# A graph-network kernel on one core: edge counts built in groups of 18 targets instead of 25, one PSUM bank each, five steps' low one-hots in one instruction

## What is computed

```python
h = relu(layernorm(x)); x = x + relu(segment_sum((h @ W0)[src] * edge_weight, dst))        # layer 0
h = relu(layernorm(x)); x = x + relu(segment_sum(norm * (h @ W1.T + b1)[src], dst))        # layer 1, norm from degrees
h = relu(layernorm(x)); x = x + relu((h + segment_sum(h[src], dst)) @ G1 + g1) @ G2 + g2   # layer 2
h = relu(layernorm(x)); x = x + attention over each node's edges, 8 heads of 64            # layer 3
```

## Time and profile before

| | us |
|---|---|
| runs shown | 3061.95, 3048.1, 3062.45 (median 3061.95) |
| the profiled execution's own time | 3038.2 |
| its span, first to last instruction | 3036.9 |
| PE matmuls busy in the span | 2486.5 (82%) |
| VectorE busy | 1823.3 (60%) |
| ScalarE busy | 568.3 (19%) |
| GpSimd busy | 966.9 (32%) |
| granted TensorE clock, mean | 0.914 of full speed |

### The profile page before, as it was taken

How to read it: one execution, slowest core, us unless ns; L and a number is a source line. 1 busy time by engine, 2 the same in 40 slices (tenths; PEclk the granted TensorE clock), 3 DMA queues, 4 the chain that set the end, 5 groups by cost and what they waited for, 6 DMA issues and landing times.

```text
span 3036.9 us, 38594 instructions
## 1 busy us (share of the span) xinstructions
PE 2486.5 (82%) x10085; PEld 1423.8 (47%) x10085; DVE 1823.3 (60%) x4888; ACT 568.3 (19%) x946; POOL 966.9 (32%) x1004
## 2 busy tenths in 40 slices
PE   7888888788777779999899999981288598888777
PEld 5544444434444445666555655640277443333332
DVE  7756577685788884665343334440266377777666
ACT  4533310000255440000000000010266100000000
POOL 0466666666100000000000000017400466666665
PEclk9899998899888889999999999985599689999999
DMA  6686656656231113446211121111134467776665
GB/s 160 185 239 178 176 164 173 171 168 185 76 104 53 62 54 86 113 110 178 76 55 52 52 62 56 34 52 29 43 116 125 125 176 206 207 236 193 190 195 171
DMA packets 154302, 386.19 MB, mean 127 GB/s; under 512 B 43712, under 2 KB 45113, under 8 KB 154115
## 3 DMA queue, kind: packets, MB, share of 16 engines
q0 software_dynamic: 74368, 232.68, 27.0%
q1 hardware_dynamic: 79064, 149.75, 17.1%
q10 hardware_dynamic: 683, 1.28, 0.2%
HBM read 330.88 MB, written 52.72 MB: 126 GB/s over the span
## 4 chain that ended last, share of the span: by engine, by line
PE 52%; DVE 21%; issue 10%; another core or an unknown queue 7%; DMA 6%; POOL 2%; ACT 1%; SPq 0%; ACTq 0%; DVEq 0%
PE banks L1845 18%; PE banks L1983 15%; PE banks L1811 7%; DVE spare L1035 4%; PE banks L2160 3%; DVE spare L1034 3%; PE banks L1975 3%; DMA ring<-edge_counts 3%; POOL ring L2331 2%; DMA ring<-table,src_t 2%; DVE sel L1108 2%; PE banks L1800 1%; DVE rstd L888 1%; PE banks L2063 1%
## 5 line engine op out<-in xcount | busy, mean ns | idle before, releaser
L1845 PE MATMUL banks<-ring,sel 128*125 128x512 f32 x1682 | 877.2, 649 | 156.6 <-issue 112.4
L2264 POOL DMA_INDIRECT ring<-table,src_t x440 | 435.2, 989 | 243.6 <-issue 104.4
L2298 POOL DMA_INDIRECT big<-score_table,src_t x104 | 98.4, 946 | 1291.2 <-DMA score_table<-node_scores 1256.0
L1845 PEld LDWEIGHTS banks<-ring,sel 128*125 128x125 f32 x1682 | 283.0, 196 | 466.6 <-issue 463.6
L2331 POOL DMA_INDIRECT ring<-table,src_t x401 | 384.8, 960 | 226.2 <-issue 98.6
L1983 PE MATMUL banks<-acc,ring 125*125 125x512 f16 x1900 | 438.2, 381 | 7.0 <-issue 7.0
L1975 PE MATMUL banks<-spare 128*125 128x325 f16 x1080 | 276.0, 370 | 73.4 <-DVE spare L1035 20.7
L1983 PEld LDWEIGHTS banks<-acc,ring 125*125 125x125 f16 x1900 | 257.1, 137 | 160.5 <-issue 27.4
L1587 DVE TENSOR_TENSOR ring<-ring,banks 128x512 f32<-128x512 f32 x388 | 255.4, 682 | 119.3 <-DMA ring<-table,src_t 91.9
L1975 PEld LDWEIGHTS banks<-spare 128*125 128x125 f16 x1080 | 152.0, 147 | 197.5 <-issue 194.9
L1436 DVE TENSOR_REDUCE big<-banks 128x16 f32<-128x448 f32 x168 | 101.6, 619 | 198.3 <-remote 139.9
(11 more groups left out here) (409 smaller groups left out, 2936.9 us busy)
## 6 DMA issues: line engine op xcount, KB each, us to landing
ring<-edge_counts SPq DMA_DIRECT2D x38, 683.6 KB
edge_counts<-big SPq DMA_DIRECT2D x25, 683.6 KB
ring<-table,src_t POOLq DMA_INDIRECT x841
sel<-edge_counts SPq DMA_DIRECT2D x12, 683.6 KB
acc<-dst_places SPq DMA_DIRECT2D x28, 256.0 KB
x<-dst_places SPq DMA_DIRECT2D x27, 256.0 KB
table<-stage SPq DMA_DIRECT2D x25, 224.0 KB
x<-in_x SPq DMA_DIRECT2D x25, 224.0 KB
```

The source lines that it names most:

```text
L1845: last = P.matmul(to, sel[:, n % SELS, :], rows, start=False, stop=True, skip_group_check=True)
L2264: G.indirect_dma_start(out=ring[:, i % RING, :], out_offset=None, in_=table[0][:, :], in_offset=bass.IndirectOffsetOnAxis(ap=src_t[:, i:i ...
```

## The change

- GT = 7 groups for each tile, of 18 targets and a last one of 17: 175 groups, 590 steps (BRS, the steps of one of five rows of step tables, 118 instead of 108).
- The key one-hot is 25 x 18 = 450 wide and fits one bank: one matmul a step. Four single banks in turn (MADE = 4) instead of two pairs.
- HOTS = 10. The low one-hots lie side by side; VectorE makes five steps' of them in one TENSOR_TENSOR of 5 x 125 against `low_t` of five steps, with a semaphore of its own, `low_ok`, for which PE waits at every fifth step.
- PE loads its registers GROUP_STEPS = 10 steps at a time, since 590 is no multiple of 20.
- ScalarE counts 174 boundaries (34 first, 14 after each tile), loads 7 registers for each tile, and copies and zeroes 450 columns (18 or 17 of every 18 copied).
- The boundaries' biases (two instructions instead of one) and the rooms of the group tables move.

```diff
-    GT = 5
-    GW_N = TN // GT
+    GT = 7
+    GW_N = -(-TN // GT)
+    GW_LAST = TN - (GT - 1) * GW_N
...
-    HALF_W = HALF_S * GW_N
-    KEY_W = 2 * HALF_W
-    HOTS = 7
+    KEY_W = TILES * GW_N
+    HOTS = 10
+    GROUP_STEPS = 10
+    MADE = 4
...
-    COUNTS_FIRST, COUNTS_EACH = 24, 10
+    COUNTS_FIRST, COUNTS_EACH = 34, 14
...
-        key_hot = [flat_spare[:, n * HOT_W:n * HOT_W + KEY_W // 2].bitcast(F16) for n in range(HOTS)]
-        low_hot = [flat_spare[:, n * HOT_W + KEY_W // 2:(n + 1) * HOT_W].bitcast(F16)[:, 0:TN] for n in range(HOTS)]
+        key_hot = [flat_spare[:, n * KEY_W // 2:(n + 1) * KEY_W // 2].bitcast(F16) for n in range(HOTS)]
+        low_room = flat_spare[:, HOTS * KEY_W // 2:HOTS * KEY_W // 2 + HOTS * TN // 2].bitcast(F16).rearrange("p (n i) -> p n i", i=TN)
+        low_hot = [low_room[:, n, :] for n in range(HOTS)]
...
-            return banks[:, 2 * n:2 * n + 2, 0:HALF_W]
+            return banks[:, n % MADE, 0:KEY_W]
...
-                V.tensor_scalar(out=low_hot[j % HOTS], in0=low_names, scalar1=low_t[:, j:j + 1], scalar2=None, op0=ALU.is_equal).then_inc(hot_ok, 1)
+                if j % LB == 0:
+                    if j >= HOTS:
+                        V.wait_ge(built, j - HOTS + LB)
+                    V.tensor_tensor(low_room[:, j % HOTS:j % HOTS + LB, :], low_names[:, None, :].to_broadcast([128, LB, TN]),
+                                    low_t[:, j:j + LB, None].to_broadcast([128, LB, TN]), ALU.is_equal).then_inc(low_ok, 1)
...
-                    pair = made_bank((n + 1) % 2)[0:TN]
-                    A.copy(made16[t % MAKES][0:TN, :, :, q * GW_N:(q + 1) * GW_N], pair.rearrange("p h (s r) -> p h s r", r=GW_N)).then_inc(taken, 1)
-                    if n + 2 >= GROUPS:
+                    made = made_bank(n + 1)[0:TN]
+                    width = GW_N if q < GT - 1 else GW_LAST
+                    A.copy(made16[t % MAKES][0:TN, :, q * GW_N:q * GW_N + width], made.rearrange("p (s r) -> p s r", r=GW_N)[:, :, 0:width]).then_inc(taken, 1)
+                    if n + MADE >= GROUPS:
...
-                if j % LOADED_TILES == 0:
-                    P.reg_load(tile_regs, group_row[0:1, j:j + LOADED_TILES])
+                if j % GROUP_STEPS == 0:
+                    P.reg_load(tile_regs[0:GROUP_STEPS], group_row[0:1, j:j + GROUP_STEPS])
...
-                P.wait_ge(hot_ok, 2 * (j + 1))
+                P.wait_ge(hot_ok, j + 1)
+                if j % LB == 0:
+                    P.wait_ge(low_ok, j // LB + 1)
                 P.wait_ge(room, v)
-                for h in range(2):
-                    to = banks[0:TN, bass.ds((v & 1) * 2 + h, 1), 0:HALF_W].rearrange("p a d -> p (a d)")
-                    last = P.matmul(to, low_hot[j % HOTS], key_hot[j % HOTS][:, h * HALF_W:(h + 1) * HALF_W],
-                                    start=False, stop=True, skip_group_check=True)
-                last.then_inc(built, 1)
+                to = banks[0:TN, bass.ds(v & (MADE - 1), 1), 0:KEY_W].rearrange("p a d -> p (a d)")
+                P.matmul(to, low_hot[j % HOTS], key_hot[j % HOTS], start=False, stop=True, skip_group_check=True).then_inc(built, 1)
```

More of the change, by code:

```diff
@@ L99, in build @@
     LOADED_TILES = 20
[L100 removed]
+    assert BRS * BRB == BSTEPS and 0 < GW_LAST <= GW_N and KEY_W <= 512 and BSTEPS % GROUP_STEPS == 0 and E // CE == CHUNKS - 1 and TILES == 5 * HQ
     Z_NORM = (D + 1.3) ** 0.5
@@ L254, in build @@
         acc16 = flat_acc.bitcast(F16).rearrange("p (t c) -> p t c", c=2 * D)
-        made16 = [big[:, n * MAKE_W:(n + 1) * MAKE_W].bitcast(F16).rearrange("p (h s r) -> p h s r", h=2, r=TN) for n in range(MAKES)]
+        made16 = [big[:, n * MAKE_W:(n + 1) * MAKE_W].bitcast(F16)[:, 0:TILES * TN].rearrange("p (s r) -> p s r", r=TN) for n in range(MAKES)]
         slot16 = [flat_ring[:, n * SLOT_W:(n + 1) * SLOT_W].bitcast(F16)[:, 0:TILES * TN] for n in range(SLOTS - 1)]
@@ L285, in build @@
         place_of_tile, tile_product = (flat_spare[:, n * gsq:(n + 1) * gsq].rearrange("p (a b) -> p a b", b=TILES) for n in range(2))
-        gap = 2 * gsq
+        gap, each = 2 * gsq, GROUPS + 1
         first_n = flat_spare[:, gap:gap + GROUPS + 1]
-        steps_n, chunk_p, steps_p, end_p, first_p, shift_p, base_p = (
-            flat_spare[:, gap + (n + 1) * 128:gap + (n + 1) * 128 + GROUPS] for n in range(7))
-        first_i = flat_spare[:, gap + 8 * 128:gap + 8 * 128 + GROUPS + 1].bitcast(I32)
-        prior = flat_spare[:, gap + 9 * 128:gap + 9 * 128 + GROUPS]
+        first_i = flat_spare[:, gap + each:gap + 2 * each].bitcast(I32)
+        steps_n, chunk_p, steps_p, end_p, first_p, shift_p, base_p, prior = (
+            flat_spare[:, gap + (n + 2) * each:gap + (n + 2) * each + GROUPS] for n in range(8))
         begun_g, weighed_g = (flat_spare[0:BRS, n * BRB * GROUPS:(n + 1) * BRB * GROUPS].rearrange("p (b g) -> p b g", g=GROUPS) for n in range(2))
-        assert BRB * GROUPS == gsq and gap + 10 * 128 <= 6 * D - EROW
+        assert 2 * BRB * GROUPS <= gap + 3 * each and gap + 10 * each <= 6 * D
         sums = [spare[0:TN, n, :] for n in range(2)]
@@ L652, in vector_program @@
             own.mark(V.tensor_copy(gstep_f[:, :], gstep_i[:, :]))
-            V.tensor_scalar(out=group_bias, in0=node_iota[:, 0:GROUPS - 1], scalar1=-float(GW_N), scalar2=0.5 - GW_N, op0=ALU.mult,
-                            op1=ALU.add).then_inc(consts, 1)
+            starts = group_start.rearrange("p (t q) -> p t q", q=GT)
+            own.mark(V.tensor_scalar(out=starts, in0=node_iota[:, 0:TILES, None].to_broadcast([128, TILES, GT]), scalar1=-float(TN), scalar2=0.5,
+                                     op0=ALU.mult, op1=ALU.add))
+            V.wait_ge(v_own, own.n)
+            V.scalar_tensor_tensor(out=starts, in0=node_iota[:, None, 0:GT].to_broadcast([128, TILES, GT]), scalar=-float(GW_N), in1=starts,
+                                   op0=ALU.mult, op1=ALU.add).then_inc(consts, 1)
             def step_tables():
@@ L1955, in tensor_program @@
             P.wait_ge(keys_ok, BRB + 1)
-            for pair in (1, 0):
-                P.matmul(bank[2 * pair][0:TN, 0:HALF_W], zeros, wide[:, 0:HALF_W], start=True, stop=True)
-                P.matmul(bank[2 * pair + 1][0:TN, 0:HALF_W], zeros, wide[:, 0:HALF_W], start=True, stop=True).then_inc(room, 1)
+            for v in range(1, MADE + 1):
+                P.matmul(bank[v % MADE][0:TN, 0:KEY_W], zeros, wide[:, 0:KEY_W], start=True, stop=True).then_inc(room, 1)
             for j in range(BSTEPS):
-                if j % LOADED_TILES == 0:
-                    P.reg_load(tile_regs, group_row[0:1, j:j + LOADED_TILES])
+                if j % GROUP_STEPS == 0:
+                    P.reg_load(tile_regs[0:GROUP_STEPS], group_row[0:1, j:j + GROUP_STEPS])
                 if j == 16:
```

21 lines of the change are left out of this document (11 added, 10 removed).

## The result

| | before | changed |
|---|---|---|
| median of the runs taken side by side, us | 3058.38 (4 runs, 3048.1 to 3062.45) | 3105.4 (4 runs, 3094.92 to 3106.03) |
| the profiled execution's own time | 3038.2 | 3094.92 |
| count stage, first to last step | 791.1 to 1144.6: 353.5 | 811.5 to 1198.5: 387.0 |
| TensorE's register loads in it | 27, 42.6 us | 59, 122.5 us |

The ratio is 1.0151 [1.0116, 1.0186]: 47 us slower, where +82 was predicted. Of the 57 us between the two profiled executions the count stage holds 33.5, its later start 20, and the rest of the program 3.

A forecast was written before the change was run, and what follows sets the result against it. TensorE's instruction queue was taken to bound the count stage: 236 + 12 + 26 + 141 + 15 = 430 us against 354, +76, and +6 before it, +82 on a median of 3,061.95 made 3,144 us; range 3,060 to 3,170.

The forecast's parts named there:

- rival B: Count stage: long loads cost a fixed surcharge, 2.66 us each; stage 368, in all +20 us, 3,082; chance 0.11.
- The bound: Count stage: TensorE's instruction queue is the bound, at about 0.54 us a step in the kernel before.
- Steps at 0.40, 0.14 for the second matmul: Count stage: one matmul fewer saves 0.14 us a step; 590 steps at 0.40 make 236 us, 56 less.
- The new wait, +12: TensorE's queue: every fifth step also waits on low_ok, 118 instructions of about 0.10 us, +12 us.
- Register loads, 26 + 141 = 167: TensorE's 59 loads of ten: 30 short at 0.88 us, 29 long at 4.86; from 38 to 167 us.
- What lengthens them: TensorE loads of 2.5 to 2.97 us occur where they meet ScalarE's loads; +3 us.
- Left over, 15: Count stage: four banks remove 11.6 us of zeroing waits, the other 12 stay, meeting loads add 3; together 15.
- VectorE hidden: Count stage: VectorE needs 0.39 us a step, 233 plus 11 us, below the stage's 430; costs nothing.
- ScalarE hidden: Count stage: ScalarE's copies and loads take 267 us, below the stage's 430; hidden.
- Before the stage, +6 within 0 to 12: Stage before the count: VectorE's longer permutations add 8.4 us, partly absorbed; +6 us, bounds 0 and 12.
- A: Count stage: loads of ten are cheap on TensorE, 26 us in place of 141; stage 315, run 3,029; chance 0.20.
- C: Count stage: wide one-hots lose their quick form and VectorE becomes the bound; stage 440, run 3,155; chance 0.05.

The follow-up runs named there:

- e2: Kernel before, with TensorE's register loads cut from 20 to 10 steps and nothing else; 3128.36 us, ratio 1.0217 to the kernel before.
- e1: Changed kernel, with TensorE loading 20 steps' registers at a time instead of 10; 3032.67 us, ratio 0.9923 to the kernel before.
- e7: e1, with each matmul of 450 columns cut into two of 225; 2777.2 us, ratio 1.0217 to the kernel before.
- e5: Changed kernel, with TensorE's registers loaded in 88 loads of 1 to 20 and ScalarE's loads as in e3; 2780.82 us in one run.
- e3: e1, with ScalarE's group ends 8 apart, so each load begins on a multiple of 32 bytes; 3031.76 us, ratio 0.9918 to the kernel before.
- e6: e1, with narrow one-hots made step by step again and no wait for low_ok; 2686.47 us, ratio 0.9885 to the kernel before.
- e8: e1, with the group tables' pieces beside every third gather step instead of every second; 2694.9 us, ratio 0.9921 to the kernel before.
- e4: Changed kernel with extra register loads for measuring, which left no instruction in the profile, so the changed kernel once more; 3106.52 us in one run.
- e12: Changed kernel, unchanged, on the third chip; 2773.93 us, ratio 1.0213 to the kernel before.

## Why the prediction was right, and where not

The direction held, as did the reason for it: the loads of ten, half of them off a boundary of 16 bytes, in a stage bound by TensorE's queue. e2 shows that they alone are worth 67 us of stage, e1 that without them the change wins 0.8%. The time of 3,144 was too high, 3105 lies inside the range. That it lies there clear of "no difference" is partly luck. The stage grew by 33.5 us where +76 was forecast, and two costs that were in no term made up for some of it: 20 us by which stores lengthen loads, and 14 us or more before the stage. With undisturbed loads (102 us) the stage would have been some 367 us, the 368 of rival B. Point by point, in its order:

- **The bound.** Right. e7 gives back two matmuls of the same columns, and the stage goes from 315 to 386 us.
- **Steps at 0.40, 0.14 for the second matmul.** Right: 0.397 at the median, 0.124 for the matmul in e7, 234 us for 236.
- **The new wait, +12.** Right: 118 x 0.106 = 12.5.
- **Register loads, 26 + 141 = 167.** The place rule was right; the long kind was mis-sized, and this is the step that failed worst: 4.8 us was ScalarE's 2.39 for five, made a rate of 0.48 per register and put on TensorE. TensorE has 0.235 per register, 2.41 for ten (e5). ScalarE's own loads of seven registers read 3.06, so that 0.48 was no rate on ScalarE either: two registers more cost 0.67 us there. The lower bound for the long kind, 2.4, is in number what came. The short kind was 1.08 and not 0.82, since a rest of two registers is two accesses and not one. What was left out goes the other way: 30 x 1.08 + 29 x 2.41 = 102 us are the undisturbed loads, and 20 us more are loads that meet stores, up to 4.08. So 167 became 126.
- **What lengthens them.** Wrong. The prediction put the 2.5 to 2.97 us of the earlier trace rows down to meetings with ScalarE's loads and priced them at +3. e3 is against it: with those at 0.55 us the same nine loads stay long. It is transfers that they meet, in the kernel before as well: the DMA engines were 0.75 busy at 234 GB/s during the load of 2.97 us at 987.5, and idle during the next one of 1.36. In the kernel before this was 6 us, in the changed one 20.
- **Left over, 15.** 14 in sum, but not by its parts. The 11.6 us of waits for zeroed banks that were to go were mostly load time, counted a second time, and so are the 26.2 us in the changed kernel. What four banks alone give was not tried; neither kernel has waits for zeroed banks of any size to take away. What is left over is steps between the loads that take more than the median.
- **VectorE hidden.** Right for the changed kernel: 0.810 us for the five-step instruction (0.806 forecast), 0.333 for a wide one-hot, and more waiting for TensorE than before. Its bound of some us of alternation, if the loads were cheap, holds too: of the 16 us by which e6 beats e8, some 4 are that, and 12.5 are the new wait.
- **ScalarE hidden.** Right: e3 takes 51 us of its loads away and gains 1.6 in the stage.
- **Before the stage, +6 within 0 to 12.** Wrong. The first pair of profiles shows +20, the first chip of the experiments +14 (802.1 in e2, whose program is the kernel before up to there, and 815.9 to 816.3 in e1, e3 and e4), the third +22.8. The sign that was named for it came true: the stretch from 417 us on grew by 15, not under 12. Of the 22.8 the tables are 6 to 7, near the 6 forecast, and the other 14 to 16 were in no term: the rows of the group fetches grew with BRS, and the prediction costed instructions that were added and not those whose size the change alters. That the pair of profiles reads 57 us and the medians 47 has to do with the profiled run before, 3038.2, which lies 10 us below the lowest of the timed ones.
- **The rivals.** A (cheap loads) falls by the rows of 2.41 us; e1 shows what it would have been, 0.8% faster. Its break-even of 2.0 us per long load fits: they average 85.0 / 29 = 2.93, and the change is slower. B (a surcharge) named 2.66 us and +20, the nearest number, by a form that e5 excludes. C (VectorE the bound) falls in the changed kernel: the wide one-hots kept their 0.333 us.

The Trainium skill (DMA: Bandwidth & Descriptors, Latency and other measured facts) puts a tensor_load's floor at about 600 ns. The trace does not agree for small loads, where e5 has 0.31 us for one register and 0.34 for four, and the 2.41 us of ten are four times that floor.
The Trainium skill (Runtime: NRT & Kernel Launch, Instruction fetch mechanics) has some 200 ns for each register also in bulk, and speaks there of the preamble's loads, while these come from SBUF. Off a multiple of 16 bytes the trace nearly agrees, with 0.235 us per register; on it, twenty registers take 1.36 us, 0.068 each.

## What to carry to other kernels

Register loads stood on TensorE's queue in full here (73.4 us less of them was 71.8 us less of stage in e1), so look at how many registers each takes and where it begins: twenty from a multiple of 16 bytes cost 1.36 us and ten from beside one 2.41, and changing 20 to 10 with the rest untouched cost 2.2% of the whole kernel. When an engine is bound by its queue, count instructions with their waits and not columns, and read a new constant through to every instruction that takes its size from it, a gather's rows among them. A rate read from one size on one engine is a bound and not a price for another. When single instructions are long at places that repeat, lay the DMA traffic beside them. And idle time in a list of waits may be an instruction on the engine's own queue: look for one inside the wait before calling it a wait for another engine.

## What the runs showed that was not expected

- A load of ten registers takes 2.41 us, but 15 of 29 such loads in the changed kernel took 2.54 to 4.08, and the same ones in each execution (e4, e12). Loads of 20 go from 1.36 to up to 3.0 at fixed steps. In all 14 traces the lengthened ones had transfers of the hardware DMA queue in flight. What a load and a transfer share is open.
- Seven registers on ScalarE, 3.06 us off the boundary and 1.35 on it; five and eight both 0.55 on it.
- An indirect gather of 118 rows takes 1.64 us of GpSimd and 5.3 us to land, one of 108 rows 1.01 and 3.2; the fifth in a row was held 6.4 us.
- One VectorE instruction for five steps in place of five is 8 us less of VectorE's busy time and 16 us more of stage, most of it the 0.106 us that its own semaphore costs TensorE's queue every fifth step.
